# Attention stage of a fused transformer block: the normalised tokens move a batch ahead into two homes, two of four query-tile pairs move into their own batch, and the routing operands of two token groups move to PSUM

## What is computed

```python
x = x + 0.5 * ffn(layernorm(x))
x = x + attn(layernorm(x))
x = x + 0.5 * ffn(layernorm(x))

def attn(x):                       # per batch of 1024 tokens, d = 128
    Q, K, V = x @ Qw, x @ Kw, x @ Vw
    s = Q @ K.T / sqrt(d) + causal_mask
    return softmax(s) @ V

def ffn(x):                        # 8192 tokens, 16 experts of 64, top 4 in the best 2 of 4 groups
    scores = sigmoid(x @ Wg.T)     # routed by scores + bias_corr, weights renormalised, times 2.5
    hid = relu(x @ W1[e].T) ** 2
    return sum_e cw[:, e] * (hid @ W2[e].T) + relu(x @ Ws1.T) ** 2 @ Ws2.T
```

## Time and profile before

| | |
|---|---|
| median of three runs | 709.67 us |
| the profiled execution | 709.15 us, of it 707.2 us span |
| first feed-forward | up to about 263 us |
| attention | about 263 to 467 us |
| second feed-forward | from about 467 us |
| busy over the span | PE 644.9, DVE 577.7, ACT 569.7, POOL 537.6 us |
| busy from 360.6 to 382.8 us (one batch) | ACT 18.68, DVE 18.24, PE 18.16, POOL 14.09 us |

### The profile page before, as it was taken

One profiled execution on the slowest core, in us unless ns is written; L12 is line 12 of the kernel. 1 busy time (PEld: TensorE's weight loads), 2 busy tenths in 40 slices (PEclk: granted clock), 3 DMA queues, 4 the chain that ended last, 5 costly groups with the idle time before them and its releaser, 6 DMA issues.

```text
span 707.2 us, 15309 instructions
## 1 busy us (share of the span) xinstructions
PE 644.9 (91%) x3395; PEld 500.1 (71%) x3395; DVE 577.7 (82%) x2597; ACT 569.7 (81%) x1198; POOL 537.6 (76%) x427
## 2 busy tenths in 40 slices
PE   4789999999999997888888778689999999999997
PEld 4567777777777766676766666567777777777775
DVE  5998989898889895677687768988989898898863
ACT  3588889889888878888798767548898888888885
POOL 3389889989899876676556645547888998898885
PEclk9999999999999998899999999999999999999999
DMA  9857676677757712664555446953887778867783
GB/s 246 192 124 158 150 161 138 138 155 157 149 122 158 164 38 47 111 105 92 89 110 107 94 80 121 200 124 65 174 166 168 156 171 177 172 137 163 160 184 77
DMA packets 129305, 97.30 MB, mean 138 GB/s; under 512 B 80992, under 2 KB 94960, under 8 KB 129264
## 3 DMA queue, kind: packets, MB, share of 16 engines
q1 hardware_dynamic: 127056, 96.24, 66.6%
q10 hardware_dynamic: 2208, 0.59, 0.4%
HBM read 72.70 MB, written 5.24 MB: 110 GB/s over the span
## 4 chain that ended last, share of the span: by engine, by line
PE 38%; DVE 13%; ACT 5%; issue 4%; POOL 3%; DMA 1%; POOLq 0%; DVEq 0%; ACTq 0%; SPq 0%
PE psum L1319 10%; PE psum L1320 9%; PE psum L1321 9%; DVE raw_max L1190 4%; ACT zn L738 2%; PE psum L1392 2%; DVE x_sb L1223 1%; DMA wb<-scratch 1%; PE psum L1350 1%; POOL shared L518 1%; PE psum L1404 1%; PE psum L1543 1%; PE psum L1544 1%; PE psum L1545 1%; DVE s_sb L1059 1%
## 5 line engine op out<-in xcount | busy, mean ns | idle before, releaser
L430 POOL TENSOR_TENSOR shared_r<-shared,shared_r 128x512 fp32r<-128x512 f32 x256 | 326.7, 1299 | 54.2 <-ACT shared L614 51.9
L1059 DVE SCALAR_TENSOR_TENSOR s_sb<-psum,wb 128x512 f32<-128x512 f32 x256 | 175.6, 688 | 48.0 <-PE psum L1321 23.8
L614 ACT ACTIVATE shared<-s_sb 128x512 f32<-128x512 f32 x288 | 178.0, 620 | 23.1 <-DVE s_sb L1059 23.0
L613 ACT ACTIVATE shared_r<-s_sb 128x512 fp32r<-128x512 f32 x256 | 159.9, 624 | 42.0 <-DVE s_sb L1059 40.8
L518 POOL TENSOR_TENSOR shared<-s_sb,shared 128x128 f16<-128x128 f32 (+3 forms) x64 | 81.9, 1281 | 73.1 <-ACT shared L544 72.6
L1319 PE MATMUL psum<-x_hi,w_hi 128*128 128x512 f32 x288 | 127.9, 444 | 6.9 <-ACT s_sb L725 4.1
L1319 PE MATMUL psum<-shared_r,w_hi 128*128 128x512 f32 x256 | 115.1, 450 | 0.7 <-POOL shared_r L430 0.5
L1320 PE MATMUL psum<-x_lo,w_hi 128*128 128x512 f32 x288 | 115.4, 401 | 0.0
L1321 PE MATMUL psum<-x_hi,w_lo 128*128 128x512 f32 x288 | 114.3, 397 | 0.0
L1321 PE MATMUL psum<-shared_r,w_lo 128*128 128x512 f32 x256 | 101.4, 396 | 0.0
L1320 PE MATMUL psum<-shared_r,w_hi 128*128 128x512 f32 x256 | 101.1, 395 | 0.0
(11 more groups left out here) (198 smaller groups left out, 1387.7 us busy)
## 6 DMA issues: line engine op xcount, KB each, us to landing
wb<-scratch SPq DMA_DIRECT2D x128, 512.0 KB, 8.1
out<-x_sb SPq DMA_DIRECT2D x16, 256.0 KB, 9.9
x_sb<-in_L_attn_x SPq DMA_DIRECT2D x4, 256.0 KB, 6.1
scratch<-wT SPq DMA_DIRECT2D x32, 32.0 KB, 1.9
w_raw<-in_L_ffn_W ACTq DMA_DIRECT2D x1, 512.0 KB, 5.8
w_raw<-in_L_ffn_W SPq DMA_DIRECT2D x1, 512.0 KB, 6.8
w_raw<-shared SPq DMA_TRANSPOSE x32, 2.9
wb<-shared SPq DMA_TRANSPOSE x32, 3.9
```

The costliest lines, as they stand in the source:

```text
L430: nc.gpsimd.tensor_tensor(g_lo[:, j % RING, :], g_f[:, j % RING, :], g_hi[:, j % RING, :].bitcast(F32), ALU.subtract).then_inc(F.glo_done, 1)
L613: nc.scalar.activation(g_hi[:, j % RING, :], s_sb[:, j % RING, :], ACT.Square)
L614: nc.scalar.activation(g_f[:, j % RING, :], s_sb[:, j % RING, :], ACT.Square).then_inc(F.sq_done, 1)
L1059: ins = nc.vector.scalar_tensor_tensor(s_, h_, 0.0, wb[:, u, c, :], ALU.max, ALU.mult)
```

## The change

- **Two homes for the normalised tokens.** `zn` becomes a list of two: the old tile, and a part of `wb`. `normalise_tokens(b + 2)` now runs whole, eight instructions, behind tile 0 of batch b; `stats` and `mean` of batch b+3 at tiles 5 to 7 of batch b, the power `attention_inv(b + 3)` before `prob_lo` of tile 7, `shift_by(b + 2)` behind the row maximum of tile 0.
- **16-bit parts on POOL alone.** ACT's `z16_hi` is gone; POOL's `z16_halves` makes a 16-bit copy and then the remainder, behind `prob_lo` of tiles 0 and 1 (in batch 0 four times, at tiles 1, 2, 4 and 5).
- **Pairs 0 and 1 of `mix`** run in their own batch, at tiles 6 and 7; the second half of `values` and of `finish` moves to tiles 0 and 1 two batches later; row sums get a third home.
- **The product of the next batch** uses one PSUM bank for both steps, so `score` of tiles 4 and 5 waits for `q_lo_part` of the next batch, and DVE runs the second `q_lo_part` ahead of the row maximum of tile 4.
- **Groups 0 and 1** of the second feed-forward route with operands in PSUM bank 5; ACT normalises all four tiles of groups 0 to 2; all slots `k` of transposes, logits, routing and powers move.
- **The end**: lead products 0 and 1 go ahead of the last exponential, and the first lead gate ahead of the last but one `finish`.

```diff
-        zn = sb("zn", [P, QT, D])
+        zn_own = sb("zn", [P, QT, D])
+        zn = [zn_own, wb[:, 0].rearrange("p c n -> p (c n)")[:, QT * D:2 * QT * D].rearrange("p (t d) -> p t d", t=QT)]
...
-        on_sb, on_ps = RouteTiles(rt_sb[:]), RouteTiles(v_ps)
+        on_sb, on_ps, on_spare = RouteTiles(rt_sb[:]), RouteTiles(v_ps), RouteTiles(tr_ps)
...
@@ POOL @@
-                    if (b, t) == (B - 6, 0):
+                    if (b, t) == (B - 6, 1):
                         inv(0)
-                    if (b, t) == (B - 3, 2):
+                    if (b, t) == (B - 5, 1):
                         inv(1)
...
+                def z16_halves(b, half):
+                    pool.wait_ge(A.zn_done, 2 * b + half + 1)
+                    wait(pool, A.mix_done, 4 * (b - 2))
...
+                    nc.gpsimd.tensor_copy(z16[:, 0, ts, :], z).then_inc(A.z16hi_done, 1)
                     pool.wait_ge(A.z16hi_done, 2 * b + half + 1)
+                    nc.gpsimd.tensor_tensor(z16[:, 1, ts, :], z, z16[:, 0, ts, :], ALU.subtract).then_inc(A.z16lo_done, 1)
...
-                        if t == 5 and b + 2 < B:
-                            attention_inv(b + 2)
+                        if t == QT - 1 and b + 3 < B:
+                            attention_inv(b + 3)
                         prob_lo(b, t)
+                        if b == 0 and t in (1, 2):
+                            z16_halves(0, t - 1)
+                        if b == 0 and t == 2:
+                            attention_inv(2)
+                        if b == 0 and t in (4, 5):
+                            z16_halves(1, t - 4)
+                        if 0 < b < B - 1 and t < 2:
+                            z16_halves(b + 1, t)
@@ ACT @@
-                            if b + 2 < B and t >= 6:
-                                normalise_tokens(b + 2, t - 6)
+                            if t == 4 and b == 0:
+                                normalise_tokens(2)
+                            if t == 0 and 0 < b < B - 2:
+                                normalise_tokens(b + 2)
@@ DVE @@
+                            if t == 4 and 0 < b < B - 1:
+                                q_lo_part(b + 1, 1 - u, 1, prep_ps(b + 1, 1))
                             row_max(b, t, u)
...
+                            if t == 0 and 0 < b < B - 2:
+                                shift_by(b + 2)
+                            if t == 1 and b > 1:
+                                finish(b - 2, 1)
...
-                        if n < 2 and k == (-31, -4)[n]:
+                        if n < 3 and k == (-30, -22, 7)[n]:
                             norm_shift(n)
@@ PE @@
+                            if t in (6, 7) and b > 0:
+                                mix(b, t - 6)
```

More of the change, by code:

```diff
@@ L790, in run @@
                         sc.wait_ge(A.pT_in[r], 16 * 2 * B)
-                    for c in range(AHEAD - 1):
+                    lead_ffn(0)
+                    start_ffn(17)
+                    for c in range(1, AHEAD):
                         lead_ffn(c)
                     uT_copy(B - 1, 1)
-                    lead_ffn(AHEAD - 1)
                 return begin, run
@@ L921, in route @@
                     score = scores[:, u]
-                    T = home(g, PREP - 2)
-                    first_on_ps = PREP - 1 if phase == 1 else 0
+                    T = on_spare if phase == 1 and isinstance(g, int) and g < UN else on_ps
+                    first_on_ps = UN if phase == 1 else 0
                     def do(ins):
@@ L1498, in z_transpose @@
                     for t in range(HQ):
-                        ins = nc.tensor.transpose(dst[:, t * P:(t + 1) * P], zn[:, half * HQ + t, :], ident[:])
+                        ins = nc.tensor.transpose(dst[:, t * P:(t + 1) * P], zn[b % 2][:, half * HQ + t, :], ident[:])
                     ins.then_inc(A.t_done, 1)
@@ L1547, in mix, with foreign @@
                         ins.then_inc(A.mix_done, 1)
+                def foreign(b):
+                    wait(pe, N1.xf_done, {3: 1, 5: 2}.get(b, 0))
+                    wait(pe, N1.sig_done, {4: 1, 6: 2, 8: 3}.get(b, 0))
+                    wait(pe, N1.wT_done, {7: 1}.get(b, 0))
                 def values(b, half):
@@ new lines, in run @@
+                            if b == 0 and t in (4, 5):
+                                q_product(1, 1, t - 4, prep_ps(1, t - 4))
+                            if 0 < b < B - 1 and t < 2:
+                                pe.wait_ge(A.exp_done, QT * b + t - 1)
+                                z_transpose(b + 1, 1 - u, t, prep_ps(b + 1, t))
+                            if b == 1 and t == 0:
+                                mix(0, 0)
+                                mix(0, 1)
+                            if t == 0 and b > 1:
+                                foreign(b)
+                                values(b - 2, 1)
@@ new lines, in run @@
+                            if t == 2 and b > 0:
+                                mix(b - 1, 2)
+                            if t in (2, 3) and 0 < b < B - 1:
+                                q_product(b + 1, 1 - u, t - 2, prep_ps(b + 1, t - 2))
+                            if t == 3 and b > 0:
+                                values(b - 1, 0)
+                            if t in (4, 5) and b > 0:
+                                mix(b - 1, 3, t - 4)
+                            if t in (6, 7) and b > 0:
+                                mix(b, t - 6)
@@ L1607, in run @@
                             if b > 0:
                                 start_ffn((b - (B - 2)) * QT + t)
-                    b, u = B - 1, (B - 1) % UN
-                    mix(b, 0)
-                    mix(b, 1)
+                    b = B - 1
+                    foreign(B)
+                    values(b - 1, 1)
+                    pe.wait_ge(A.exp_done, QT * B - 1)
+                    lead_ffn(0)
+                    lead_ffn(1)
+                    start_ffn(16)
                     pe.wait_ge(A.exp_done, QT * B)
-                    lead_ffn(0)
+                    lead_ffn(2)
```

235 lines of the change are left out of this document (102 added, 133 removed).

## The result

The changed kernel takes **724.28 us** (median of 4 runs, 723.46 to 724.73), the kernel before beside it on the same chip 709.21 us (4 runs): a ratio of 1.0213, 95% interval 1.0195 to 1.023, slower by 15.1 us. The profiled execution has a span of 722.6 us against 707.2, 15.4 more. One launch of the kernel before, made later beside some of the experiments, took 813.31 us at a granted clock of 0.75, and no figure here counts it. The forecast was 718 with a range of 702 to 726 and a chance of 0.70 for slower.

The account below looks back on a forecast made before the run. It took a ring through four engines (score, row maximum, exponential, 16-bit copy, `prob_lo`) as the bound, no engine being full. 5.1 + 9.2 - 3.5 - 2.5 = +8.3 us on 709.15 gave 717.5, forecast 718 us, range 702 to 726.

Parts of the forecast that it names:

- Clean batch: A batch without extra group work: ACT's own 17.6 us plus five idle stretches, 24.1 us in all.
- term (1), the shift: Before the eight normalisations: the shift waits out POOL's `prob_lo` of tile 7, and ACT stands 2.8 us.
- Term (2), the block: Eight normalisations on ACT, 3.25 us in one block; tiles 2 and 3 wait some 0.5 us for the chain behind it.
- Term (3), `q_lo`: Ahead of tile 4's row maximum DVE does `q_lo`, which needs ACT's `q_hi`; ACT waits 1.8 us.
- Terms (4) and (5): `finish` between tiles 4 and 5 on DVE, 0.8 us; then tile 6's score after it, 0.6 us.
- Batches 2 and 3: At tile 2 DVE waits in `norm_shift` for a group's power on POOL: 4.0 us more, 28.1 us each.
- Six batches: Batch 1 to batch 7, between row maxima of tile 1: 154.7 us, +9.2 us.
- Batch 0: POOL's work delays the normalisations; tile 1 of batch 1 comes at 298.0 instead of 292.9 us, +5.1 us.
- Batch 7: Routing in PSUM no longer stalls beside `prob_lo`, and group 2's first parts leave the batch: -3.5 us.
- The end: Two lead products run in PE's pause and the first gate waits less: -2.5 us (ends 0 and -4).
- no gain at the end: Rival: lead gates wait for the weights' broadcast or PE for DVE as before; +6, 724 us; chance 0.12.
- the shift gets in first: Rival: shift starts before POOL's long `prob_lo` and takes 0.18, not 2.1 us; 15.7 less, 702 us; chance 0.19.

Follow-up runs that it names:

- the power first: Changed kernel, but powers of feed-forward groups 0 and 1 stand on POOL behind tile 0 of batches 2 and 3, not tile 1: 721.08 us.
- the pairs back: Changed kernel with the first two pairs of every batch's product moved back behind tile 0 of the next batch: 725.17 us.
- `q_lo` behind: Changed kernel, but DVE takes the row maximum of tile 4 ahead of the second low part of the next product, as before: 727.68 us.
- three single gains: Changed kernel with token means in PSUM, group powers a tile earlier, or statistics, power and shift a batch earlier: 714.32, 721.08, 716.33 us; together 705.97 us.
- the groups' shifts: Kernel with all three edits, plus shifts of feed-forward groups 0 to 2 reading means from PSUM and some steps a tile later: 701.33 us.

## Why the prediction was right, and where it was off

The direction, the place and the main mechanism held; the sum was 6 us short, and the measured time lies near the upper end of a wide range. In the profiled launches it is 15.4 against the +8.3 worked out: batch 0 came out 1.8 lower, the six batches 5.4 higher, batch 7 1.4 and the end 2.3 higher, and 0.2 was gained ahead of batch 0. By its own steps:

- **Clean batch, term (1), the shift: right.** 2.8 us of ACT's idle time worked out (with 5.7 us where the three instructions give 5.6), 2.65 measured at the seam shown, 2.26 to 2.65 at all five; the shift 2.1 us worked out, 2.08 measured. The runs show the cause: 7.5 us less when this alone is taken away. In the rule of the Trainium skill that the prediction named (SBUF — State Buffer, the two separate sides) only a DVE instruction with two SBUF inputs, or in a two-port mode, contends; the shift with its mean in PSUM is outside it, and the 0.17 us beside a `prob_lo` of 2.52 agree.
- **Term (2), the block: mis-sized, the largest miss.** 0.5 us worked out; ACT stood 1.7 us before tile 3's exponential (at 305.06) in batches 1, 4 and 5. The prediction said that PE and DVE "run ahead and then have nothing", priced only 0.5 us behind that, and took it that PE's time is not what the ring waits for. Here it was: PE's 5.2 us of idle time were followed by 3.9 us at half clock, on products that the ring waits for, and moving half of `z_hi` ahead of the block gave 5.1 us back. Splitting the block itself was not tried.
- **Term (3), `q_lo`: the size right, the reason incomplete.** ACT waited 1.67 to 2.10 us there (1.8 worked out), but not because DVE took the wrong one first, as `q_lo` behind showed.
- **Terms (4) and (5):** 0.8 + 0.6 worked out, 0.91 + 0.77 measured in batch 1.
- **Batches 2 and 3: the sum right by luck, two errors that cancel.** 28.1 worked out each; from block to block they took 27.3 and 29.3 us, 28.3 in the mean. The clean batch under them was too small: from block to block batches 1 and 4 took 26.4 and 26.3 us, not 24.1. The 4.0 us on top were too large: 0.8 and 2.9 were found, and with the power first only 2.0 of the 8 us came back. The order of events held: DVE stood 2.33 us, then the shift lasted 0.86. One part of the 4.0 is the cast, 0.61 us instead of the 1.17 that the sum took (ends 0.43 and 1.3), 1.1 us less for two. The estimate of 0.77 from the Trainium skill (GPSIMD Engine Reference, section 3.1) was nearer, and also too high; the 1.8 cycles per element that it is worked out from stand there as the best case of a tight loop, beside a dearer two-input one, and a cast has no price there.
- **Six batches:** +9.2 worked out, +14.6 measured. Batches 1 (28.6 us between the maxima instead of 24.1) and 5 (26.5 instead of 24.9) hold it. For batch 1 the cut at tile 1's maximum misleads a little: its own block began with the maximum of tile 1 (296.1), the next one 2.1 us ahead of it (322.6), and from block to block it took 26.4, still 2.3 above the 24.1.
- **Batch 0: +5.1 worked out, +3.3 measured.** Two casts of 1.17 that lasted 0.61 are 1.1 of the difference; the power began at 278.6 instead of 281.2.
- **Batch 7: -3.5 worked out, -2.1 measured,** and not by the first half of the reason: routing in PSUM gave nothing there (16.0 us with it back in SBUF, 16.2 in the change). Group 2's first parts, which left the batch, are what remains of it; that was not tried by itself.
- **The end: -2.5 worked out, -0.2 measured.** Here the rival "no gain at the end" was right in kind. Its time, 724 us, equals the measured one by luck: it put +6 us on the end, where 2.3 were missing, and the batches made up the rest. In the changed kernel a shift of a group stands there 2.47 us for its power and then 2.08 beside a `prob_lo` (timeline of DVE):

```profile
476.29 2.08 DVE L905 SCALAR_TENSOR_TENSOR shift<-rt_sb,roots 128x4 f32<-128x4 f32 x1 [2.47 <-POOL roots L414]
```

Whether that is what took the gain was not tried. It stays open.
- **Moved pairs at zero: held,** within what was measured (0.7 us slower with the pairs back, intervals overlapping).
- The rival in which the shift gets in first did not occur (6 of 7 lost). Of its 15.7 us, 10.6 were for five shifts; at 2.1 less 0.18 us each they are 9.6, and the run that makes these five short, with the epsilons, gave 8.8. Its other terms were not tried by themselves.

## What to carry to other kernels

Work moved "a batch ahead" can cost more than it gives if its issue stands as one block in front of the ring's next member (here, with the shift's wait at the seam, 28 us against 13): look at what each engine has behind the block, and treat idle time of TensorE as a cost where matmuls on the path follow it. Price a tiny DVE instruction with both inputs in SBUF, next to long GpSimd ones, at up to the GpSimd instruction's duration (here 2.08 us for 8 columns). An operand in PSUM took that away, for 16 columns of a bank, but it saves time only where the instruction is last on a path. Try such edits one by one and then together: here three single gains added up and turned a change that cost 2.1% into one 0.4% faster than the kernel before, 1.2% with the groups' shifts.

## What the runs showed of the hardware that was not expected

- The one-input epsilon (SBUF to SBUF, 8 columns) stands still beside GpSimd as well: up to 1.69 us, and 0.167 with its input in PSUM. The rule of the Trainium skill used above (SBUF — State Buffer, the two separate sides) includes it if it ran in a two-port mode, which no row here shows.
- GpSimd didn't pay for the meeting: `prob_lo` of tiles 7 and 0 took 2.51 us beside the waiting shift and 2.52 beside the short one.
- The granted clock went from 0.87 over a stretch with no matmul at all (4.9 us) to 0.50 in the 3.9 us of work after it, and with 1.44 us of matmuls put into that stretch it was still 0.50 after it.
- A cast of 512 columns from 32 to 16 bits on GpSimd takes 0.61 us, about half of the subtraction on as many (1.16):

```profile
L516 POOL CAST zn<-zn x6: 610/612/614, 274.2 to 411.2; 128x512 f16<-128x512 f32 x6
```
